# Two score products of a vision-transformer layer in the other order on TensorE

## The reference

```
h = relu(x0 @ W0.T) * (x0 @ W1.T) @ Wo.T            # token part, per image (512 x 256)
h = concat(cls_tok, h)                              # 513 tokens
q, k, v = bitlinear(layernorm(h), w_q / w_k / w_v)  # int8-like input, ternary weights
s = q @ k.T / 4                                     # 16 heads of 16, 513 x 513
h = h + bitlinear(softmax(s) @ v, w_o)
# then 8 experts, top 2 of each token, silu(gate) * up, down
h = h + moe(layernorm(h))
```

## Time and profile before

| | |
|---|---|
| median of three executions | 2406.64 us |
| the profiled execution | 2407.87 us |
| its span | 2406.0 us |
| TensorE matmul busy | 2069.0 us (86%) |
| TensorE weight load busy | 1061.3 us (44%) |
| VectorE busy | 1573.6 us (65%) |
| ScalarE busy | 1211.6 us (50%) |
| GpSimd busy | 910.8 us (38%) |

### The profile page before, as it was taken

How to read it: one execution, slowest core, us unless ns; L and a number is a source line. 1 busy time by engine, 2 the same in 40 slices (tenths; PEclk the granted TensorE clock), 3 DMA queues, 4 the chain that set the end, 5 groups by cost and what they waited for, 6 DMA issues and landing times. The chain is left out here.

```text
span 2406.0 us, 46759 instructions
## 1 busy us (share of the span) xinstructions
PE 2069.0 (86%) x11964; PEld 1061.3 (44%) x12049; DVE 1573.6 (65%) x4036; ACT 1211.6 (50%) x2360; POOL 910.8 (38%) x894
## 2 busy tenths in 40 slices
PE   4789999899898898998999989871099999999997
PEld 2333444443343443443344433321066666666665
DVE  4477898887887887887888898841633333333332
ACT  1256566566555665665656666650444444434443
POOL 2222242332323423333333234133245555555554
PEclk9899999999999999999999998985599999999999
DMA  2322322322222322223222232201533333333332
GB/s 90 91 67 58 89 87 70 93 72 84 74 80 68 84 72 83 83 70 88 67 81 81 66 85 73 66 27 57 180 48 55 56 53 55 54 54 55 52 55 36
DMA packets 181072, 171.87 MB, mean 71 GB/s; under 512 B 40002, under 2 KB 169620, under 8 KB 180884
## 3 DMA queue, kind: packets, MB, share of 16 engines
q1 hardware_dynamic: 150612, 134.81, 19.4%
q0 software_dynamic: 30272, 34.80, 9.1%
HBM read 100.70 MB, written 68.93 MB: 71 GB/s over the span
## 5 line engine op out<-in xcount | busy, mean ns | idle before, releaser
L1148 DVE TENSOR_REDUCE mxs<-bank 128x1 f32<-128x512 f32 x1024 | 697.0, 684 | 199.9 <-PE bank L494 186.3
L824 ACT ACTIVATE pt<-bank 128x512 f32<-128x512 f32 x1024 | 589.0, 593 | 385.9 <-PE bank L503 383.5
L494 PE MATMUL bank<-ks,qs 96*128 96x512 bf16 x1024 | 401.5, 393 | 89.9 <-DVE mxs L1148 70.4
L503 PE MATMUL bank<-qs,ks 99*128 99x512 bf16 x1024 | 397.3, 389 | 8.9 <-ACT pt L824 8.4
L1698 POOL DMA_INDIRECT out<-y_sb,ids x136 | 214.6, 1578 | 272.6 <-DMA out<-y_sb,ids 194.9
L512 PE MATMUL bank<-pt,v_sb 128*32 128x512 f32 x2048 | 280.8, 621 | 0.0
L494 PEld LDWEIGHTS bank<-ks,qs 96*128 96x128 bf16 x1024 | 103.5, 101 | 359.7 <-DVE mxs L1148 247.4
L975 POOL DMA_INDIRECT list_dram<-pay,slot_i x130 | 138.3, 1064 | 253.2 <-DVE pay L1273 218.7
L1823 DVE TENSOR_TENSOR hid_e<-bank,act_g 128x512 f32<-128x512 f32 x136 | 94.1, 692 | 210.2 <-PE bank L1744 210.2
L1827 DVE TENSOR_TENSOR hl<-bank,hh 128x512 bf16<-128x512 f32 x136 | 94.1, 692 | 210.2 <-ACT hh L1797 210.2
L1744 PE MATMUL bank<-gu_l,xh 128*128 x544 | 206.7, 380 | 23.0 <-issue 21.5
(11 more groups left out here) (283 smaller groups left out, 3519.0 us busy)
## 6 DMA issues: line engine op xcount, KB each, us to landing
qs<-qk_dram SPq DMA_DIRECT2D x128, 128.0 KB, 2.5
ks<-qk_dram SPq DMA_DIRECT2D x64, 192.0 KB, 3.2
xt<-x_t SPq DMA_DIRECT2D x16, 512.0 KB, 4.1
h_dram<-h_sb SPq DMA_DIRECT2D x16, 512.0 KB, 3.8
qs<-qk_dram SPq DMA_DIRECT2D x128, 64.0 KB, 2.2
ks<-qk_dram SPq DMA_DIRECT2D x64, 128.0 KB, 3.2
hw<-h_dram SPq DMA_DIRECT2D x16, 512.0 KB, 4.5
out<-hw SPq DMA_DIRECT2D x16, 512.0 KB, 3.0
```

The lines of the kernel that those rows point to most:

```text
L494: mm(score[u % 2][:, :], qs[0:QK, h, blk(t)], ks[0:QK, h, :], start=True, stop=True) \
L503: mm(scoret[u % 2][:, :], ks[0:QK + MROWS, h, blk(t)], qs[0:QK + MROWS, h, :], start=True, stop=True).then_inc(s("pe_st"), 1)
L824: f(pt[:, t % 2, j, :], scoret[u % 2][:, :], ACT.Exp).then_inc(s("act_exp"), 1)
L1148: v.reduce_max(mxs[:, t, g * GH + j:g * GH + j + 1], score[u % 2][:, :], AX.X).then_inc(s("dve_mx"), 1)
```

## The change

In every slot of every step TensorE issues the transposed score product ahead of the score product. Nothing else is changed: the waits, banks, signals and the other engines' programs are the same.

```diff
                     at = UNITS * g + u
+                    if st[0].ok:
+                        scoret_unit(*st, u)
                     if C.ok:
                         score_unit(C, g, u)
-                    if st[0].ok:
-                        scoret_unit(*st, u)
                     if u == 3 and tg[0].ok:
                         pv(*tg, TB - 1)
```

## The result

The changed kernel took 2418.04 us (median of five; before 2406.64, a median of five as well, not of three). One of the five executions of the changed kernel took 4215.62 us; it counts in that median and is left out of the ratio. The ratio of the two is 1.0048 with a 95% interval of 1.0029 to 1.0068: slower by 11.4 us, between 7 and 16. The profiled execution took 2418.04 us, its span is 2416.2 us, 10.2 us more than before.

A forecast was written before the change was run, and what follows sets the result against it. Neither TensorE (91% busy) nor VectorE (84%) alone was the bound, but a two-way hand-over; 4.4 + 0.8 + 0.4 + 8.4 = 14.0 us on 2407.87 gave 2421.9, stated as a median of 2421 us, range 2400 to 2438.

The forecast's parts named there:

- The sum: Whole kernel: delays of 4.4, 0.8, 0.4 and 8.4 us add to 14.0 us on 2407.87 us.
- Slots 6 to 9: Score products behind the late exponential's wait and slot 8's transposed product delay slot 9 by 0.44 us, in ten images: 4.4 us.
- Slots 26 to 30: Slot 28's score product, behind the wait for slot 26's exponential, delays line 772 by 0.61 us; 14 images, 8.4 us.
- Its signs: New trace: score products of slots 26 to 30 some 0.6 us longer, slot 28's maximum waiting about 0.8 us, slots 46-53 unchanged.
- +0.22, given back at S(46): Slot 30's row maximum waits 0.22 us more for its score product; regained at slot 46's score product.
- sooner by 0.22 at the entry, later by 0.22 at the exit: zero: Slots 46-47: long product starts 0.22 us sooner, the next score product VectorE awaits comes 0.22 later; they cancel.
- Entries and exits through X: zero: TensorE's work other than the two score products, such as transposes waiting for VectorE's result: no shift.
- Lap images: Images 5, 7, 9, 11 behind a lap's branch: slot 8's transposed product first costs 0.2 us each, 0.8 us.
- No change: Rival: rotation wholly absorbed, exponentials of slots 4 and 26 coming sooner; 2407 us, chance 0.15.
- Slower throughout: Rival: every score product VectorE waited for comes 0.22 us later, 247 times, 54 us; 2462 us, chance 0.08.
- Faster: Rival: the transposed product fills TensorE's 107 waits for row maxima, 0.22 us each; 2384 us, chance 0.10.
- The clock: Rival: each image catches one more low-clock stretch, 26 us; with the sum 2448 us, chance 0.05.

The follow-up runs named there:

- e1: The changed kernel run again unaltered in a later session, against the kernel before: 2420.1 us against 2398.9, ratio 1.0091.
- e11: The changed kernel run a third time unaltered, against the kernel before: 2420.64 us against 2401.23, ratio 1.0086.
- e3: Kernel before with the transposed score product first only in slots 6 and 28: 2410.57 us against 2398.9, ratio 1.0056.
- e4: Kernel before with the transposed score product first only in slots 46, 53 and 63: 2397.15 us, ratio 0.9996.
- e10: Kernel before with the transposed score product first only in slots 46 and 57: 2405.75 us against 2409.12, ratio 0.9988.
- e9: Changed kernel with the score product first again in slots 0, 6, 8, 19, 28, 30, 47, 48, 58: 2414.3 us against 2409.12 before, 1.0018.
- e5: The kernel before, unaltered, profiled a second time: 2401.03 us against 2401.29, ratio 1.0004.

## Why the prediction was right, and where it wasn't

- *The sum.* 14.0 us were forecast; 11.4 were measured at first, 21.2 in e1 and 19.4 in e11. The fixed part of the profiles is 18.5 us. That 14.0 lies near the first result is in part luck: the sum left out about 0.33 us in each image (0.22 and 0.11, below) and the waits of slot 35, 1.5 us in all, and knew nothing of the chance terms, -8 us in slots 35 to 53 of the first pair of profiles.
- *Slots 6 to 9* (0.44 in ten images): the size is right, 0.43 to 0.46 in nine of them (0.26 in image 14), the path only in part. The prediction added 0.22 at T(6) and 0.22 at T(8), both through M(8)'s wait for S(8). M(8) has no such wait in the changed kernel; the delay already comes from M(6)'s 0.60 us wait for S(6), and e3 has 0.40 of the 0.43 us without T(8) ahead. That the two prices, which overlap, seemed to add up is luck.
- *Slots 26 to 30* (0.61 for line 772): right in images 2 to 14. From the transposes of line 648 in slot 9 to line 772 in slot 29 the shift grows by 0.73 in image 10, of which 0.11 arose in slot 20; e3 alone gives 0.62. In image 1 T(28) doesn't wait. In images 1 and 14 T(35) does, 0.41 and 0.73 us; this is the 1.5 us of S30-S35, which the prediction lacked.
- *Its signs.* S(26) to S(30) was to be 0.6 us longer or more and M(28) to wait about 0.8 us; measured are 0.43 and 0.55 us. The change also makes the transposes of slot 25 wait 0.11 us, so S(26) itself comes 0.19 us later, which the first projection takes up in a wait of 0.34 us that it had before; and M(27) is late too. Slots 46 to 53 are unchanged to 0.16 us, but for the clock, and so is the expert phase, as forecast.
- *"+0.22, given back at S(46)"*: this is the step that failed. S(46) does free the long product 0.22 us sooner, but S(47) behind it is then late by 0.22 again, as the prediction itself said one part earlier ("sooner by 0.22 at the entry, later by 0.22 at the exit: zero"). The gain was booked twice. The table has no -0.22 in S46-S53, and of S(30)'s shift nothing comes back: 0.22 us in 14 images, 3 us.
- *"Entries and exits through X: zero"*: it missed that M(19) late by 0.22 makes line 1299 late and with it line 554: 0.11 us in each image. The exit through S(10) is in the S9-S26 column, and is the 0.22 that S(30) then hands to VectorE.
- *Lap images* (0.2): S0-S9 was +0.24 in image 5 and +0.02, -0.57, -0.53 in the others, which also hold a changing stretch of low clock behind the branch. The size can't be read there.
- *Rivals.* "No change" had E(4) and E(26) end sooner; they end as late as before, and T waits 12.2 us. "Slower throughout" would be 54 us. "Faster", T filling the waits for M, was tried alone in e4 and e10: 1.8 and 3.4 us less, both intervals with 1.000 in them. "The clock" didn't add a low stretch per image; slots 46 to 53 had fewer (images 3 and 11 instead of 5, 10, 12 and 14).

## What to carry to other kernels

In this kernel swapping two instructions of a queue cost next to nothing where both were ready: 55 slots of 64 together about 5 us (e9), two others 11.7 us (e3). It costs where the one that goes first can be late (then the other inherits the wait) and where the other is what an idle engine waits for: count those places in the timeline and multiply. A rotation of a loop's order moves each shift along until a wait takes it up; book each gain at one wait only, and don't add two delays of one chain before a run has had each alone. And profile the unchanged kernel twice before explaining a difference of a microsecond.

## What the runs showed of the hardware

- VectorE operations of 0.15 to 0.19 us can take 0.65 to 2.05 us beside a GpSimd tensor operation, and then end 0.02 to 0.05 us behind it. They need not: in the short form L1242 and the two operations behind it took 0.18, 0.19 and 0.28 us beside L992, which took 0.70 us itself instead of 0.63. Slots 35 to 46 took 16.7 or 17.7 us for it.
- The low clock behind a wait of TensorE comes and goes between executions of one program. Slots 46 to 53 of image 12 took 12.24 us at a granted clock of 0.86 in the first profile of the kernel before and 10.58 us at 1.00 in e5. Behind the lap's branch, 3.94 us of idle TensorE, the changed kernel's first product takes 0.61 us instead of 0.38; in e1's profile of the same kernel three of the four such products took 0.39 us, behind waits of 3.99 to 4.05 us:

```profile
1137.78 0.61 PE L503 MATMUL bank<-qs,ks 99*128 99x512 bf16 x1 [3.94 <-issue]
```
